# Two-layer gated cross-attention: the second layer loads a stored split of the context, and GpSimd masks ten score units of twelve there

## The reference

```python
x = x + tanh(g_xattn[0]) * attention_0(layernorm(x), ctx, ctx, mask_1x1xSxS2)   # mask shared by all sequences
x = x + tanh(g_ffn[0]) * dense_ffn(layernorm(x))
x = x + tanh(g_xattn[1]) * attention_1(layernorm(x), ctx, ctx, mask_BxSxS2)     # a mask per sequence
x = x + tanh(g_ffn[1]) * moe_ffn(layernorm(x))
# attention: q, k, v = x @ wq, ctx @ wk, ctx @ wv, 16 heads of 16
# scores = q k^T / 4, masked where mask == 0, softmax over the 375 keys, times v, projected by wo
```

## Time and profile before

| | us |
|---|---|
| median of 3 runs | 1806.68 (1806.5 to 1809.34) |
| profiled execution, own time | 1801.03 |
| its span, first to last instruction | 1799.0 |
| TensorE busy | 1509.3 |
| VectorE busy | 1081.4 |
| GpSimd busy | 848.6 |
| ScalarE busy | 800.7 |
| mean granted TensorE clock | 0.921 of full speed |

### The profile page before, as it was taken

The page is one execution under the profiler, slowest core; times in us unless marked ns, Lnnn a source line. Parts: engine busy times, 40 slices in busy tenths (PEclk is TensorE's granted clock), DMA queues, the critical chain, the costliest instruction groups (busy, mean ns, idle before and its releaser), DMA issues. The chain is left out here.

```text
span 1799.0 us, 40766 instructions
## 1 busy us (share of the span) xinstructions
PE 1509.3 (84%) x15271; PEld 1089.3 (61%) x15271; DVE 1081.4 (60%) x3493; ACT 800.7 (45%) x1822; POOL 848.6 (47%) x794
## 2 busy tenths in 40 slices
PE   1739999999997799999957379999999995509996
PEld 0317777777775356655633157777777774507775
DVE  4727777777774455555437267777777763515663
ACT  3316666666664222222213146666666652114441
POOL 1347777777775000000013447777777761064332
PEclk9959999999998899999988589999999996559999
DMA  7654454444430212222127545665565622035440
GB/s 230 220 105 96 95 111 105 97 104 107 100 80 20 59 59 64 69 91 60 33 76 224 95 106 122 126 117 116 113 128 116 110 45 69 26 120 171 134 149 17
DMA packets 225378, 183.62 MB, mean 102 GB/s; under 512 B 70314, under 2 KB 218735, under 8 KB 225192
## 3 DMA queue, kind: packets, MB, share of 16 engines
q1 hardware_dynamic: 219560, 171.36, 40.1%
q0 software_dynamic: 5632, 9.78, 1.7%
HBM read 99.53 MB, written 48.49 MB: 82 GB/s over the span
## 5 line engine op out<-in xcount | busy, mean ns | idle before, releaser
L947 ACT ACTIVATE probs_a<-bank 125x448 f32<-125x448 f32 x768 | 387.9, 541 | 27.4 <-PE bank L807 11.3
L697 POOL TENSOR_TENSOR probs_a<-probs_a,keep_a 125x448 int32<-125x448 int32 x256 | 285.0, 1135 | 122.1 <-ACT probs_a L947 121.9
L697 POOL TENSOR_TENSOR probs_a<-probs_a,mask_keep 125x448 int32<-125x448 int32 x256 | 285.1, 1135 | 105.6 <-ACT probs_a L947 105.4
L1021 DVE CUSTOM_DVE_ANT_0 masked_scores_a<-bank,mask_add_a 112x375 bf16<-112x375 f32 x512 | 259.4, 546 | 111.1 <-PE bank L778 107.2
L1021 DVE CUSTOM_DVE_ANT_0 masked_scores_a<-bank,mask_add 112x375 bf16<-112x375 f32 x512 | 259.3, 546 | 92.2 <-PE bank L778 88.6
L778 PE MATMUL bank<-k_stack_a,q_stack_a 96*128 96x375 f16 x1024 | 292.5, 327 | 9.6 <-issue 3.0
L807 PE MATMUL bank<-q_stack_a,k_stack_a 97*128 97x224 f16 x1536 | 252.4, 259 | 11.2 <-DMA q_stack_a<-max_t_a 10.3
L1335 PE MATMUL bank<-h0h_f,ffn_w 128*128 128x448 f16 x512 | 180.7, 353 | 10.8 <-DVE h0l_f L1214 10.8
L807 PEld LDWEIGHTS bank<-q_stack_a,k_stack_a 97*128 97x128 f16 x1536 | 145.8, 98 | 71.3 <-DMA q_stack_a<-max_t_a 11.8
L1335 PE MATMUL bank<-h0l_f,ffn_w 128*128 128x448 f16 x512 | 180.5, 353 | 0.0
L1174 POOL DMA_DIRECT2D x_after_ffn<-y_f x8 | 5.9, 741 | 344.7 <-DVE y_f L1221 344.7
(11 more groups left out here) (201 smaller groups left out, 3121.5 us busy)
## 6 DMA issues: line engine op xcount, KB each, us to landing
k_stack_a<-k_high_a SPq DMA_DIRECT2D x256, 96.0 KB, 4.1
ctx_in_a<-in_ctx_dram SPq DMA_DIRECT2D x64, 375.0 KB, 3.4
w_in_e<-in_L_ffn_W_dram SPq DMA_DIRECT2D x16, 1024.0 KB, 8.4
k_stack_a<-k_low_a SPq DMA_DIRECT2D x128, 96.0 KB, 4.3
q_stack_a<-q_split SPq DMA_DIRECT2D x128, 84.0 KB, 3.3
x_and_bias<-xb_q SPq DMA_DIRECT2D x16, 448.0 KB, 4.4
q_split<-high_q SPq DMA_DIRECT2D x32, 224.0 KB, 3.8
x_sum_a<-x_and_bias SPq DMA_DIRECT2D x64, 112.0 KB, 4.2
```

The source lines that it names most:

```text
L697: pool.tensor_tensor(bits, bits, cols, ALU.mult).then_inc(masked, 1)
L947: act.activation(probs[:, i, :], score_bank[i % 3][0:CK, 0:GT], ACT.Exp, scale=DK ** -0.5).then_inc(exped, 1)
L1021: dve.tensor_tensor_reduce(masked_scores[:, use_of[x.value, h] % 3, :], bank_of(x, h)[0:S, 0:S2], mask_add[x.four][:, 0:S2], 1.0, -LARGEST ...
```

## The change

Layer 0 stores the high and low parts of every sequence's context to a new tensor in device memory, behind its load of queries. Layer 1 has no `ctx_in`, no copies on ScalarE and no subtractions on GpSimd; it loads both parts of sequence s behind the stores of the keys of p, and TensorE's keys wait for these loads. In layer 1 GpSimd masks ten units of the twelve (5 and 11 are left to TensorE), in layer 0 eight as before. GpSimd's first memsets in layer 1 no longer wait for a low part.

```diff
@@ -36,7 +36,7 @@
 ROW = D + 2
 NOBODY = 8192
 
-POOL_UNITS = (0, 1, 3, 4, 6, 7, 9, 10)
+POOL_UNITS = ((0, 1, 3, 4, 6, 7, 9, 10), (0, 1, 2, 3, 4, 6, 7, 8, 9, 10))
 W_SCALE = 2.0 ** 6
 MASKED = float(2 ** 30)
 EPS = 1e-5
@@ -105,6 +105,7 @@
     x2 = dram("x_after_ffn_0", [B, S, D], F32)
     based = dram("x_and_bias", [B, S, D], F32)
     q_split = dram("q_split", [2, 3, P, B * S], F16) 
+    split = dram("context_split", [B, 2, P, KC * S2], F16)
     add_1 = dram("mask_add_1", [B, S, S2], BF16)
     keep_1 = dram("mask_keep_1", [B, CK, CH, S], I32)
     expert_in = dram("expert_in", [E * CAP, ROW], F32)
@@ -136,10 +137,10 @@
         m["nobody"] = sb("nobody", [P, CAP * E * ROW // P // 14], U32)
         setup_phase(nc, m, a, expert_in)
         queries_phase(nc, m, 0, a["x"], a["mask_1x1xSxS2_ik1"], q_split, based)
-        attention_phase(nc, m, 0, based, x1, a["ctx_1024"], (m["mask_add"], m["keep"]), q_split)
+        attention_phase(nc, m, 0, based, x1, a["ctx_1024"], (m["mask_add"], m["keep"]), q_split, split)
         ffn_phase(nc, m, a, x1, x2, a["mask_BxSxS2_if1"], add_1, keep_1)
         queries_phase(nc, m, 1, x2, None, q_split, based)
-        attention_phase(nc, m, 1, based, out, a["ctx_1024"], (add_1, keep_1), q_split)
+        attention_phase(nc, m, 1, based, out, a["ctx_1024"], (add_1, keep_1), q_split, split)
         moe_phases(nc, m, a, expert_in, out)
 
 
@@ -529,7 +530,7 @@
         body(Quad(s // 4, s % 4))
 
 
-def attention_phase(nc, m, layer, x_in, x_out, context, masks, q_split):
+def attention_phase(nc, m, layer, x_in, x_out, context, masks, q_split, split):
 
 
     tag = f"_a{layer}"
@@ -546,7 +547,7 @@
 
         SPILL = P - CK
         WIDE = CH * P
-        ctx_in = many(2, sb, "ctx_in", [P, KC, S2], F32)
+        ctx_in = [] if layer else many(2, sb, "ctx_in", [P, KC, S2], F32)
         ctx_high = many(4, sb, "ctx_high", [P, KC * S2 + SPILL], F16)
         ctx_low = many(4, sb, "ctx_low", [P, KC * S2 + SPILL], F16)
         k_high, k_low = many(2, sb, "k_high", [P, KC, WIDE], F16), many(2, sb, "k_low", [P, KC, WIDE], F16)
@@ -571,7 +572,7 @@
 
         ctx_loaded, q_loaded, k_loaded = many(2, sem, "ctx_loaded"), many(2, sem, "q_loaded"), many(2, sem, "k_loaded")
         max_loaded = [many(2, sem, f"max_loaded_{half}_") for half in range(2)]
-        masks_loaded = many(4, sem, "masks_loaded")
+        masks_loaded, split_stored = many(4, sem, "masks_loaded"), many(4, sem, "split_stored")
         x_loaded, x_stored = many(2, sem, "x_loaded"), many(2, sem, "x_stored")
         pads_set, ones_set = sem("pads_set"), sem("ones_set")
         ctx_high_ready, ctx_low_ready = sem("ctx_high_ready"), sem("ctx_low_ready")
@@ -593,7 +594,7 @@
         work_bank = m["bank"][7]
         HALF = UNITS // 2
         HH = H // 2
-        pool_units = POOL_UNITS
+        pool_units = POOL_UNITS[layer]
 
         ctx_rows = context.rearrange("b (c p) k -> b p c k", p=P)
         q_rows = q_split.rearrange("e g (r p) (b t) -> e b (g r) p t", p=NP, t=S)
@@ -631,6 +632,17 @@
                 dst = q_view(n.four)[STACK:STACK + 1, NP // 2 * half:NP // 2 * (half + 1), :]
                 sp.dma_start(dst.rearrange("w p t -> w (p t)"),
                              max_t[half][:, :]).then_inc(max_loaded[half][n.two], 16)
+
+            def load_split(s):
+                old = s.back(4)
+                wait(sp, v_made, 2 * (old.value + 1) if old.exists(B) else 0)
+                for n, tile in enumerate((ctx_high, ctx_low)):
+                    sp.dma_start(tile[s.four][:, 0:KC * S2], split[s.value, n]).then_inc(ctx_loaded[s.two], 16)
+
+            def store_split(p):
+                sp.wait_ge(ctx_low_ready, KC * (p.value + 1))
+                for n, tile in enumerate((ctx_high, ctx_low)):
+                    sp.dma_start(split[p.value, n], tile[p.four][:, 0:KC * S2]).then_inc(split_stored[p.four], 16)
 
             def load_context(s):
                 old = s.back(2)
@@ -662,28 +674,36 @@
                 p, g, x, d, e = (s.back(n) for n in range(1, 6))
                 if d.exists(B):
                     store_max(d, 1)
-                if s.exists(B) and s.value + 1 < B:
+                if not layer and s.exists(B) and s.value + 1 < B:
                     load_context(s.back(-1))
                 if p.exists(B):
                     load_queries(p)
+                    if not layer:
+                        store_split(p)
                 if d.exists(B):
 
                     wait(sp, x_stored[d.two], 16 * d.use2)
                     sp.dma_start(x_sum[d.two][:, :], take(x_in, d.value)).then_inc(x_loaded[d.two], 16)
                 if p.exists(B):
                     store_keys(p)
+                if layer and s.exists(B):
+                    load_split(s)
                 if x.exists(B):
                     store_max(x, 0)
                 if e.exists(B):
                     wait(sp, summed, e.value + 1)
                     sp.dma_start(take(x_out, e.value), x_sum[e.two][:, :]).then_inc(x_stored[e.two], 16)
 
-            load_context(Quad(0, 0))
+            if not layer:
+                load_context(Quad(0, 0))
             sp.wait_ge(pads_set, 4)
             sp.wait_ge(ones_set, 4)
             run_quads(B, 5, body)
             for n in range(2):
                 sp.wait_ge(x_stored[n], 16 * B // 2)
+            if not layer:
+                for n in range(4):
+                    sp.wait_ge(split_stored[n], 32 * B // 4)
 
         @block.gpsimd
         def _(pool):
@@ -710,12 +730,13 @@
                 for i in pool_units:
                     if d.exists(B):
                         mask_unit(d, i)
-                if s.exists(B):
+                if s.exists(B) and not layer:
                     low_context(s, 0)
                     low_context(s, 1)
                 if isinstance(s.value, int) and s.value == 0:
 
-                    pool.wait_ge(ctx_low_ready, KC)
+                    if not layer:
+                        pool.wait_ge(ctx_low_ready, KC)
                     for n in range(4):
                         pool.memset(k_stack[n][STACK:P, :], 1.0).then_inc(ones_set, 1)
                         pool.wait_ge(ones_set, n + 1)
@@ -731,7 +752,10 @@
 
             def make_keys(p, g, d, e, j):
                 if j == 0:
-                    pe.wait_ge(ctx_low_ready, KC * (p.value + 1))
+                    if layer:
+                        pe.wait_ge(ctx_loaded[p.two], 32 * (p.use2 + 1))
+                    else:
+                        pe.wait_ge(ctx_low_ready, KC * (p.value + 1))
 
                     if e.value > 0:
                         pe.wait_ge(summed, e.value)
@@ -922,6 +946,7 @@
                     act.wait_ge(ctx_loaded[s.two], 16 * (s.use2 + 1))
                     old = s.back(4)
                     wait(act, v_made, 2 * (old.value + 1) if old.exists(B) else 0)
+                    wait(act, split_stored[s.four], 32 * (old.use4 + 1) if old.exists(B) else 0)
                 act.activation(ctx_high[s.four][:, c * S2:(c + 1) * S2], ctx_in[s.two][:, c, :],
                                ACT.Copy).then_inc(ctx_high_ready, 1)
 
```

## The result

The changed kernel takes 1833.32 us (median of 4 runs, 1825.09 to 1836.31) against 1806.59 for the kernel before on the same chip (median of 4 runs): ratio 1.0137, 95% interval 1.0109 to 1.0165, so 1.1 to 1.7% slower. The forecast was 1813.4 with 1797 to 1825 as its range: the sign was right, the size four times too small, and the result lies outside the range. The profiled execution took 1836.31 us, 3.0 over its median; that of the kernel before, 1801.03 us, lies 5.6 under its own.

What follows compares the result with a forecast made beforehand. It took TensorE's issue to bound both layers, with the transfer queue ahead of the maxima as layer 1's second limit. Terms +2.5 +2.2 +0 +1.5 +0.5 = +6.7 us on 1806.68 gave 1813.4 us, range 1797 to 1825.

Steps and rivals of the forecast that it cites:

- Steady stages of layer 1: 28 stages of layer 1: -0.38 us for mask matmuls and +0.47 for later maxima, net +0.09 each, +2.5 us.
- So GpSimd is hidden with 0.4 us to spare.: Layer 1 stage: GpSimd's masks end at 12.52 us, before the weighting reaches unit 10 at 12.94.
- The landing moves by 1.05 - 0.48 = +0.57 us.: Layer 1 maxima transfer: two loads ahead cost 1.05 us, the earlier head returns 0.48, so it lands 0.57 later.
- rival (a): Layer 1: the moved loads are hidden and maxima wait no longer than now; -6.4 us, 1800.3 us; chance 0.30.
- the price by five engines: Layer 1 loads: `keep`'s 125 partitions lie on 5 engines; 24 KB per engine costs 0.83 us rather than 1.05.
- The size of the maxima's wait: Layer 1: TensorE's first score unit's wait for the maxima rises from 7.8 to some 21 us over 28 stages.
- Layer 0's steady stages: Layer 0: the added stores are hidden, 0 us, up to +8 if they turn into layer 1's wait.
- The end of layer 1: Last sequence of layer 1: two more GpSimd masks with nothing to hide them push the end out by 2.2 us.
- Start of layer 1: Layer 1's start: SyncE free 6.6 us earlier against a serial chain of first loads; +0.5 us, bounds -4 and +6.
- (b): Layer 0 falls into layer 1's wait for maxima and pays its 7.8 us: 1821 us; chance 0.09.
- (c): GpSimd becomes layer 1's bound through slower masks; 0.2 us a stage beyond its cover is +5.6: 1819 us; chance 0.04.
- (d): Layer 1's stage is set by the maxima's landing alone, so removed matmuls bring nothing: 1827 us; chance 0.09.

Runs made afterwards that it cites:

- a_neg: The changed kernel with layer 1's first negation of the maxima moved from VectorE to ScalarE: 1822.98 us, ratio 1.0092 to the kernel before.
- a_eight: The changed kernel with eight instead of ten units masked by GpSimd in layer 1: 1819.40 us, ratio 1.0097 to the kernel before.
- b_keep2: The kernel before with layer 1's load of `keep` cut into 112 and 13 partitions: 1791.55 us, ratio 0.9927.
- a_best: The changed kernel with `keep` in two loads, first negation on ScalarE and the split loaded at the head of SyncE's stage: 1793.38 us, ratio 0.9924.
- b_ten_neg_keep2: The kernel before with ten units masked on GpSimd in layer 1, first negation on ScalarE, `keep` in two loads, no stored split: 1794.30 us, ratio 0.9929.

## Why the prediction was wrong

**Steady stages of layer 1 (+2.5 forecast, +29.3 measured)** is the failed term, and it failed in three steps.

1. "So GpSimd is hidden with 0.4 us to spare." The arithmetic was right: masks end 12.52 us into the stage (1172.51), and of the 28 weightings one waits for them, for 0.6 us. But the step asked only who waits for GpSimd's results. It did not ask who needs what GpSimd holds while it works. The gap of 0.31 us ahead of unit 6, which the additional mask of unit 2 fills, was where VectorE's negation ran. Price: the shortest stage 14.10 instead of 13.39, or 0.7 us in each of 28 stages, some 20 us; undone alone it gives back 12.4 in a_neg, since the maxima's wait takes the rest, and in a_eight 11.6 on top of paying for the mask matmuls again. The trace of before had the clue where the layers start and end: there the same negation takes up to 1.14 us beside GpSimd's work, and its mean of 166 ns over the steady stages hides it. The prediction has no term for VectorE at all, as no instruction of VectorE was edited.
2. "The landing moves by 1.05 - 0.48 = +0.57 us." Where TensorE waits for maxima, the first score unit comes on average 15.59 us after the start of the stage that issues them (18 stages) instead of 14.51 (11 stages): +1.08, nearly twice that. In a_eight, without the lock, it is still 15.39. The 0.48 was hardly given back, as the last key's issue ends only 0.1 us earlier (8.78 us into the stage for 8.87, both means): SyncE's waits at the stores of keys, for ScalarE, VectorE and TensorE, grew from 6.8 to 16.9 us over the layer. The prediction had said as much against rival (a) ("what leaves the head does not shorten the tail"), but not applied it to its own term. A part of the +1.08 can also come from the lock, as the maxima of these stages are issued 0.7 us later (10.80 for 10.12); no run separates the two fully. And the price by five engines, "an estimate by which the steady part would be -0.6 us" (by the half that is taken for 1.05 us it is -0.4), went the wrong way: `keep` was not an equal sharer of the 1.05 us but the reason why keys and maxima land late at all, as b_keep2 shows.
3. Half speed was not in the sum. Three waits for maxima were followed by stretches at 1.2 GHz, worth some 4.6 us. The kernel before has no such stretch in its 28 periods.

**The size of the maxima's wait** was "from 7.8 to some 21 us over the 28 stages"; it is 21.8, counted as the prediction counts it, by how much later the first units start than in a stage without a wait (7.8 before; as idle time in the profile it is 18.5 and 5.8). The number holds by luck and not by its working: it counted on stages of 13.35 us. With the stages lengthened by the lock, the same wait came from a shift twice as large; in a_neg, whose stages are as short as forecast, it is 27.

**What held.** Layer 0's steady stages: 0, exactly; its keys' last issue ends 1.0 us later (1.2 forecast) and its maxima are issued at 10.08 us as before. Layer 0's start: +1.5 forecast, +2.1 measured. The end of layer 1: +2.2 forecast for the last two masks, 2.2 measured after the last weighting, where GpSimd shows

```profile
1516.14 10.97 POOL L717 TENSOR_TENSOR probs_a<-probs_a,keep_a 125x448 int32<-125x448 int32 x10 [1.89 <-ACT probs_a L972]
```

against 8.79. The mask matmuls' worth of 0.38 us a stage: 13.39 for 13.35.

**Start of layer 1**: +0.5 forecast within -4 and +6; measured -2.8. SyncE's wait for the memsets fell by 6.3 us (17.2 to 10.9), as forecast; the start as a whole gained 2.8 of them, and the serial chain of the first loads is the forecast's reason for the rest. How much of it is the queue of `keep` was not separated; b_keep2 alone gains 6.6 us there.

**The rivals.** (a) fell: the maxima land later. (b) did not happen in the changed kernel; one stage or a few of it appear in a_eight and a_best (0.9 and 2.3 us). (c) "GpSimd becomes the bound of layer 1" had the right engine and the wrong way: GpSimd bounds it, but by holding VectorE and not by being late; in b_ten_neg_keep2, with its subtractions, it does so by being late. (d) gave the nearest number, 1827, for a reason that is not the one found. The range ended at 1825: it left out (d) by choice, no rival had the lock, and the lock, the landing and half speed came together.

## What to carry to other kernels

Before an engine is called hidden, list the small instructions of its neighbours that run in its gaps: work that fills GpSimd's last gap can hold a VectorE instruction of 0.16 us for a whole mask of 1.13 us, and a mean over the group hides it, so look at the longest one and at start-up. Look at the partition count of every transfer that lies ahead of a small urgent one: one load of 125 partitions set the landing of what was queued behind it, and cutting it into 112 and 13 was worth 0.7% of the kernel, as much as the removed matmuls could have brought (10.6 us, 0.6%). When two limits lie close together (issue, GpSimd, landing), a removed cost is paid back by the next one; here a_neg alone got back 12.4 of some 20 us.

## What the hardware showed that was not expected

- A VectorE instruction of 112 x 8 elements from on-chip memory to on-chip memory takes 1.13 us instead of 0.16 when GpSimd runs masks without a gap, and ends 25 to 31 ns after the mask; instructions with an operand in a matmul bank (reductions 0.54, normalisation 0.42) keep their durations.
- One 164 KB load of 125 partitions, instead of 112 and 13, raises the landing of the next load (112 KB) from 2.4 to 6.5 us and that of keys from 3.8 to 5.1. At most 7 or 8 of its packets are under way at a time, against 16 to 20.
- After 2.77 us of standstill TensorE ran at half speed for nearly 3 us. A wait of 1.65 us in the same layer was also followed by half speed, and in a_eight waits of up to 2.6 us were followed by full speed, so the length of a wait alone doesn't tell.
